# Window attention on one core: scores and transposes in smaller tiles of TensorE, a lag of three quarters, and two evacuations moved from VectorE to ScalarE

## The chip, the cores and the metric

The kernel runs on one core of a Trainium2 chip. The metric is the device time of one execution in microseconds (us). The kernel before takes 4781.35 us, the median of 3 runs (4780.85 to 4781.38).

## The reference

The input is 16 images of 56 x 56 places with 192 channels. Two residual layers follow one another, each on a group norm (32 groups) of its input. The first is a linear recurrence over 7 x 7 windows with a feed-forward of 768 channels; the change does not touch it. The second is shifted window attention, with 12 heads of 16 dimensions, 49 tokens to a window and 64 windows to an image:

```python
x = jnp.roll(x, (-s0, -s1), axis=(1, 2))
qkv = xw @ qkv_w.T + qkv_b
q, k, v = (qkv[0] * hd ** (-0.5), qkv[1], qkv[2])
attn = jnp.einsum('bhnd,bhmd->bhnm', q, k)
attn = attn + bias[None]          # relative position, then the shift mask
attn = jax.nn.softmax(attn, axis=-1)
out = jnp.einsum('bhnm,bhmd->bhnd', attn, v)
out = out @ proj_w.T + proj_b
```

## The kernel before

The attention works in units. A unit is a row of 8 windows of one image, so there are 128 units. A unit has four quarters p = 0 to 3, each of two windows w, laid in partitions 0 to 48 and 64 to 112 (SLOT = 64). Each engine runs the same order, written out by hand in its function `slot(i, c, r)`, joined by semaphores. The loop body holds two units (c = 0 and 1).

For a quarter, in words: **scores** (L1241) multiply queries `Q` by keys `Kp` into `ps_s`, for all heads of both windows. `Kp` is the keys spread out with zeros (block diagonal) by DMAs of SyncE (L840), so that one matmul serves several heads: four in the kernel before (HB = 4), whose 64 rows meet 4 x 49 = 196 columns. That makes 6 matmuls of a 64 x 64 tile of the array; the trace shows each fp32 matmul as two, so 12. VectorE scales them and adds the bias (L1097, into `L`), takes row maxima (L1101) and subtracts them for half the heads (L1111); GpSimd subtracts the other half (L888). ScalarE takes exponentials (L960, into `E`), VectorE the row sums and reciprocals (L1105, L1107), GpSimd multiplies (L882). Two quarters later (`lagged`) TensorE **transposes** the probabilities (L1249, 6 of 128 x 98 weights and 128 columns, both windows at once, into `ps_t`), ScalarE copies them out (L969, `PT`), TensorE multiplies them by the **values** (L1284, 98 x 32 tiles, 12 matmuls shown as 24, into `ps_v`) and ScalarE moves them out (L989, `oT`).

Between these TensorE has the work of the next unit v = u + 1 and of the last one u - 1: `turn` (L1180, transposes of the input, two halves h), `project` (L1192, queries and keys, steps 0, 1, 2 of 5 matmuls), `values` (L1204, two halves of 10) and `mix` (L1223, the output projection, two halves of 8). All share three PSUM banks `ps_w`, so each waits until its bank was read. The input parts `x_hi`, `x_lo` that `project` needs are made by ScalarE (`upper`, L930) and VectorE (`lower`, L1065). Step 0 of `project` yields keys and the last query channels; the latter are moved out by VectorE (`queries_b`, L1074), like half of the values (L1124).

TensorE's order in a unit is: p = 0: scores, transposes, mix 0, turn 0, values product, turn 1; p = 1: scores, transposes, project 0 and 1, values product; p = 2: scores, transposes, project 2, values 0, values product; p = 3: scores, transposes, values 1, values product, mix 1.

## Time and profile before

| | us |
|---|---|
| median of 3 runs | 4781.35 |
| the profiled execution | 4778.66 |
| its span, first to last instruction | 4776.7 |
| attention, first to last scores matmul | 2513 to 4759 |
| TensorE busy in the span | 4503.8 (94%) |
| VectorE busy | 3946.8 (83%) |
| ScalarE busy | 2366.2 (50%) |
| GpSimd busy | 2379.3 (50%) |

Starts in the timeline count from the first instruction. A matmul's duration runs from its start to its last result, so matmuls that follow each other overlap in the list: the pace of a group is read from starts, not from durations. Units are alike, so one unit of the steady stretch stands for all.

### The profile page before, as it was taken

Reading aid. Unit: us, or ns where it says so; the run is one execution under the profiler, and the core shown is the slowest. Engines: PE = TensorE matmul, PEld = TensorE weight load, DVE = VectorE, ACT = ScalarE, POOL = GpSimd, SP = SyncE. Lnnn points to the kernel's source line nnn. Section 1 sums busy time; section 2 is a strip of 40 time slices with the busy share of each in tenths; the row PEclk is TensorE's granted clock in tenths of the full one; section 3 lists DMA queues with packets and bytes.
Section 4 is the critical chain, followed back from the end, with each engine's and each line's share of the span. In section 5 each row is a group of like instructions: output and inputs, shape, how many; then the busy total and the mean of one; then the engine's idle time right before and its main releaser. Section 6 shows DMA issues by size and latency. Waiting matters only on the chain. (4 is left out here: it accounts for less than half of the span.)

```text
span 4776.7 us, 123308 instructions
## 1 busy us (share of the span) xinstructions
PE 4503.8 (94%) x42504; PEld 3833.8 (80%) x42504; DVE 3946.8 (83%) x7850; ACT 2366.2 (50%) x4594; POOL 2379.3 (50%) x2098
## 2 busy tenths in 40 slices
PE   0599999999999999999969999999999999999998
PEld 0488888888888888888857888888888888888887
DVE  6788888888888888888827888888888888888887
ACT  0244444444444444444415555555555656555565
POOL 1245554555555554555425555555555555555555
PEclk9999999999999999999969999999999999999999
DMA  8011111111111111111112222222222222222222
GB/s 341 21 38 39 39 41 38 38 39 39 41 37 39 39 41 37 39 40 41 34 40 67 69 68 69 69 67 71 67 70 69 68 68 69 70 68 70 67 70 59
DMA packets 397987, 285.95 MB, mean 60 GB/s; under 512 B 155355, under 2 KB 396235, under 8 KB 396747
## 3 DMA queue, kind: packets, MB, share of 16 engines
q1 hardware_dynamic: 395204, 283.19, 20.2%
q10 hardware_dynamic: 2736, 2.14, 0.1%
q8 instruction: 29, 0.48, 0.0%
q14 instruction: 18, 0.15, 0.0%
HBM read 120.34 MB, written 87.31 MB: 43 GB/s over the span
## 5 line engine op out<-in xcount | busy, mean ns | idle before, releaser
L882 POOL TENSOR_TENSOR E<-E,ri 128x588 f32<-128x588 f32 x512 | 646.3, 1262 | 1028.5 <-DVE ri L1107 1028.3
L602 PE MATMUL ps_o<-w,g_hi 128*128 128x384 f32 x2352 | 710.9, 365 | 5.9 <-DVE g_lo L542 4.1
L414 ACT ACTIVATE gF<-ps_g,b1f 128x512 f32<-128x512 f32 x588 | 404.7, 688 | 393.0 <-PE ps_g L633 390.7
L960 ACT ACTIVATE E<-L 128x588 f32<-128x588 f32 x512 | 356.1, 695 | 475.6 <-POOL L L888 242.5
L1097 DVE SCALAR_TENSOR_TENSOR L<-ps_s,bias 128x588 f32<-128x588 f32 x512 | 394.5, 770 | 178.0 <-PE ps_s L1241 161.9
L602 PE MATMUL ps_o<-w,g_lo 128*128 128x192 f32 x2352 | 534.8, 254 | 0.0
L1249 PE MATMUL ps_t<-ident,E 128*98 128x128 f32 x3072 | 441.3, 280 | 41.1 <-POOL E L882 41.1
L441 POOL TENSOR_TENSOR res<-xt,b2b 128x768 f32<-128x768 f32 x98 | 181.5, 1852 | 591.1 <-DVE x L490 591.1
L400 ACT ACTIVATE h_hi<-ps_h,hbias 128x512 fp32r<-128x512 f32 x196 | 123.1, 679 | 703.7 <-PE ps_h L617 703.7
L1249 PEld LDWEIGHTS ps_t<-ident,E 128*98 128x98 f32 x3072 | 313.4, 127 | 195.4 <-POOL E L882 108.3
L1241 PE MATMUL ps_s<-Kp,Q 64*64 64x196 f32 x6144 | 455.4, 342 | 2.7 <-DMA Kp<-K 2.7
L602 PEld LDWEIGHTS ps_o<-w,g_hi 128*128 128x128 f32 x2352 | 429.7, 189 | 26.6 <-issue 24.7
L602 PEld LDWEIGHTS ps_o<-w,g_lo 128*128 128x128 f32 x2352 | 444.0, 191 | 0.0
L1101 DVE TENSOR_REDUCE mx<-L 128x12 f32<-128x588 f32 x512 | 392.2, 766 | 17.5
L989 ACT ACTIVATE oT<-ps_v,vb 128x98 f32<-128x98 f32 (+1 forms) x1024 | 289.1, 334 | 234.6 <-PE ps_v L1284 228.7
L1105 DVE TENSOR_REDUCE sm<-E 128x12 f32<-128x588 f32 x512 | 387.8, 757 | 12.6 <-ACT E L960 1.4
L1223 PE MATMUL ps_w<-wp,oT 128*98 128x192 f32 x2048 | 385.4, 331 | 1.1 <-ACT oT L989 0.7
L1284 PEld LDWEIGHTS ps_v<-PT,Vx 98*32 98x32 f32 x12288 | 291.2, 150 | 92.9 <-issue 63.9
L1284 PE MATMUL ps_v<-PT,Vx 98*32 98x49 f32 x12288 | 351.4, 232 | 12.7 <-issue 3.9
L419 ACT ACTIVATE g_hi<-gF 128x512 fp32r<-128x512 f32 x588 | 355.4, 621 | 0.0
L451 POOL TENSOR_TENSOR g_lo<-gF,g_hi 128x512 fp32r<-128x512 f32 x196 | 250.5, 1299 | 197.3 <-ACT g_hi L419 197.3
L888 POOL TENSOR_TENSOR L<-L,mx 128x294 f32<-128x294 f32 x512 | 345.2, 674 | 6.1 <-DVE mx L1101 6.1
(211 smaller groups left out, 12090.5 us busy)
## 6 DMA issues: line engine op xcount, KB each, us to landing
xs<-in_x SPq DMA_DIRECT2D x8, 4704.0 KB, 22.0
xt<-in_x SPq DMA_DIRECT2D x98, 384.0 KB, 3.4
x_cells<-x SPq DMA_DIRECT2D x784, 48.0 KB
xb<-x_cells SPq DMA_DIRECT2D x128, 294.0 KB
Vx<-V SPq DMA_DIRECT2D x512, 73.5 KB
out<-yo SPq DMA_DIRECT2D x128, 294.0 KB
Kp<-K SPq DMA_DIRECT2D x512, 49.0 KB, 1.9
Kp<-K SPq DMA_DIRECT2D x512, 24.5 KB, 1.8
```

What stands on the lines that cost most here:

```text
L414: act.activation(gF[f % 4][:, :], ps_g[:, f % 2, :], ACT.Gelu, bias=b1f[:, f:f + 1]).then_inc(s_gelu, 1)
L419: act.activation(g_hi[:, g, :], gF[g % 4][:, :], ACT.Copy).then_inc(s_gh, 1)
L602: last = pe.matmul(dst, g[:, f, P * k:P * (k + 1)], w, start=(f == 0 and i == 0), stop=(f == FT - 1 and i == 1))
L882: pool.tensor_tensor(e, e, ri[p][:, :].unsqueeze(2).to_broadcast([P, HEADS, T]), ALU.mult)\
L960: act.activation(E[pp][:, :, :], L[pp][:, :, :], ACT.Exp).then_inc(s_ex, 1)
L1097: dve.scalar_tensor_tensor(out=L[p][:, :, :].rearrange("p (a h) m -> p a (h m)", a=3), in0=s_block(slice(0, 3)), scalar=HD ** -0.5, in1=ta ...
L1101: dve.tensor_reduce(mx[p][:, :], L[p][:, :, :], AX.X, ALU.max).then_inc(s_mx, 1)
L1105: dve.tensor_reduce(sm[pp][:, :], E[pp][:, :, :], AX.X, ALU.add).then_inc(s_sm, 1)
L1223: last = pe.matmul(ps_w(OUT1 if half else OUT0)[0:T2, C * a:C * (a + 1)], oT[d][p][:, k, :], wp[:, k, :], start=(k == 0), stop=(k == 1))
L1241: last = pe.matmul(s_block(b)[SLOT * w:SLOT * (w + 1)], Q[c][rows, chunk, 2 * p + w, :], Kp[c][rows, chunk, :, 2 * p + w, :], start=True, ...
L1249: last = pe.transpose(ps_t[0:T2, j // JB, P * (j % JB):P * (j % JB + 1)], E[lp][:, 2 * j:2 * j + 2, :].rearrange("p h m -> p (h m)"), iden ...
L1284: last = pe.matmul(ps_v[row:row + 2 * HD, col:col + T], Vx[lc][0:T2, 2 * lp + w, j:2 * HD * JP:JP], PT[lp % 2][0:T2, j, T * w:T * (w + 1)] ...
```

## The change

The head pairs become the unit of the scores: HB = 2, so a scores matmul has 32 rows of weights and 98 columns, and there are 12 for a quarter (24 in the trace) in tiles of 32 x 64. They come in two parts: pairs at places 0, 3, 1, 4 ahead of the transposes, and those at 2, 5 after them, behind a wait for the first part (`s_scx`). The transposes are split by window: 12 with 64 rows, 98 weight columns and 64 columns each. The heads lie in the order PAIR_AT in the logits and in the values product, whose loop now takes pairs 0, 4, 2, 1, 5, 3 and with them the column groups 0, 0, 2, 1, 1, 3 of the array, where it took 0, 1, 2, 3, 0, 1. The lag from scores to transposes is three quarters. `queries_b` and the copy of values half 0 go from VectorE to ScalarE. ScalarE copies `PT` ahead of the exponentials, VectorE subtracts maxima ahead of the row sums, GpSimd does `less_max` ahead of `norm`. `turn` 0 and 1 stand together in p = 0, `mix` 0 moves to p = 2, `project` 1 behind the values product of p = 1, `project` 2 and `values` 0 behind that of p = 2. The bank numbers of `ps_w` and the waits on them follow.

```diff
+PAIR_AT = (0, 4, 2, 1, 5, 3)
-HB = HEADS // 3
-QB = 256
+HB = 2
+SB = HEADS // 2 * T
-OUT0, TURN, QK, VAL, OUT1 = 0, 1, 3, 6, 8
+LAG = 3
+TURN, KEYS, OUT0, QRY, VAL, OUT1 = 0, 2, 4, 5, 6, 8
+def ps_qk(step):
+    return ps_w(QRY if step == 2 else KEYS + step)
-    return ps_s[:, :, :].rearrange("p a (b n) -> p (a b) n", n=QB)[:, b, 0:HB * T]
+def s_pair(j):
+    return ps_s[:, 2 * j // JP, T2 * (j % (JP // 2)):T2 * (j % (JP // 2) + 1)]
-    return (u, c, p - 2) if p >= 2 else (u - 1, 1 - c, p + 2)
-    return (64 * (b // 2), b % 2)
+    return (u, c, p - LAG) if p >= LAG else (u - 1, 1 - c, p + UP - LAG)
+    return slice(2 * HD * (g % PA), 2 * HD * (g % PA + 1)), g // PA
...
+            if is_unit(u):
+                less_max(u, p)
             if is_unit(pu):
                 norm(pu, pp)
-            if is_unit(u):
-                less_max(u, p)
...
+    def queries_b(i, c):
+        v = 2 * i + c + 1
+        full = ps_qk(0)[:, 0:UW].rearrange("p (w t) -> p w t", t=T)
+        upto(act, s_sc, UP * (v - 1))
+        act.activation(Q[1 - c][0:CB, 1, :, 0:T], full[CB:P], ACT.Identity,
+                       bias=par[1 - c][CB:P, 3:4]).then_inc(s_qb, 1)
...
-            if is_unit(pu):
-                k = UP * u + p - 1
-                act.wait_ge(s_sub, k + 1)
-                act.wait_ge(s_sbp, k + 1)
-                upto(act, s_pt, k - 3)
-                act.activation(E[pp][:, :, :], L[pp][:, :, :], ACT.Exp).then_inc(s_ex, 1)
+            lu, lc, lp = lagged(u, c, p)
+            k = UP * u + p - LAG
             if nxt and p == 2:
                 evacuated(i, c, 1)
-            lu, lc, lp = lagged(u, c, p)
-            k = UP * u + p - 2
             if is_unit(lu):
                 act.wait_ge(s_pt, k + 1)
                 upto(act, s_pv, k - 1)
-                act.activation(PT[lp % 2][0:T2, :, :].rearrange("p (a b) (w t) -> p a (b w) t", a=2, w=2),
-                               ps_t[0:T2, :, 0:JB * P].rearrange("p a (n t) -> p a n t", t=SLOT)[:, :, :, 0:T],
+                act.activation(PT[lp % 2][0:T2, :, :].rearrange("p j (w t) -> p w j t", w=2),
+                               ps_t[0:T2, :, 0:JP * SLOT].rearrange("p w (j t) -> p w j t", t=SLOT)[:, :, :, 0:T],
                                ACT.Copy).then_inc(s_ptc, 1)
-            if nxt and p == 1:
-                evacuated(i, c, 0)
-            if nxt and p == 2:
-                evacuated(i, c, 2)
-            if nxt and p == 3:
-                act.wait_ge(s_v, 2 * (u + 1) + 2)
-                copied(act, i, c)
-                act.activation(V[0:T2, 2:4, :], v_sum(1), ACT.Copy).then_inc(s_vc[1], 1)
-            if nxt and p == 0:
-                upper(i, c, 0)
+            if is_unit(pu):
+                act.wait_ge(s_sub, UP * u + p)
+                act.wait_ge(s_sbp, UP * u + p)
+                upto(act, s_pt, UP * u + p - 4)
+                act.activation(E[pp][:, :, :], L[pp][:, :, :], ACT.Exp).then_inc(s_ex, 1)
+            if nxt:
+                if p == 0:
+                    upper(i, c, 0)
+                    upper(i, c, 1)
+                if p == 1:
+                    evacuated(i, c, 0)
+                    queries_b(i, c)
+                if p == 3:
+                    act.wait_ge(s_v, 2 * (u + 1) + 2)
+                    copied(act, i, c)
+                    act.activation(V[0:T2, 0:2, :], v_sum(0), ACT.Copy).then_inc(s_vc[0], 1)
+                    act.activation(V[0:T2, 2:4, :], v_sum(1), ACT.Copy).then_inc(s_vc[1], 1)
             if is_unit(lu):
...
-            if nxt and p == 0:
-                upper(i, c, 1)
+            if nxt and p == 2:
+                evacuated(i, c, 2)
...
-        dve.tensor_scalar(Q[1 - c][0:CB, 1, :, 0:T], full[CB:P], par[1 - c][CB:P, 3:4], None,
...
-            if is_unit(pu):
-                dve.wait_ge(s_ex, k)
-                dve.tensor_reduce(sm[pp][:, :], E[pp][:, :, :], AX.X, ALU.add).then_inc(s_sm, 1)
-                dve.wait_ge(s_sm, k)
-                dve.reciprocal(ri[pp][:, :], sm[pp][:, :]).then_inc(s_ri, 1)
             if is_unit(u):
                 dve.wait_ge(s_mx, k + 1)
                 l = L[p][:, 0:HS, :]
                 dve.tensor_tensor(l, l, mx[p][:, 0:HS].unsqueeze(2).to_broadcast([P, HS, T]),
                                   ALU.subtract).then_inc(s_sub, 1)
-            if is_unit(u - 1) and p == 0:
-                finish(i, c, 0)
             if nxt and p == 0:
                 lower(i, c, 0)
                 lower(i, c, 1)
-            if nxt and p == 1:
-                queries_b(i, c)
-            if nxt and p == 2:
-                dve.wait_ge(s_v, 2 * (u + 1) + 1)
-                copied(dve, i, c)
-                dve.tensor_copy(V[0:T2, 0:2, :], v_sum(0)).then_inc(s_vc[0], 1)
+            if is_unit(pu):
...
+            if is_unit(u - 1) and p == 2:
+                finish(i, c, 0)
...
+    def scores(c, p, places):
+        for j in places:
+            rows, chunk = pair_rows(PAIR_AT[j])
+            for w in range(2):
+                last = pe.matmul(s_pair(j)[SLOT * w:SLOT * (w + 1)], Q[c][rows, chunk, 2 * p + w, :],
+                                 Kp[c][rows, chunk, :, 2 * p + w, :], start=True, stop=True)
+        return last
...
-        if h == 0:
-            pe.wait_ge(s_xb[d], 16 * LOADS * (i + c + 1))
-            upto(pe, s_vc[1], v)
-        else:
-            if isinstance(v, int):
-                upto(pe, s_yo, 2 * (v - 2))
...
             pe.wait_ge(s_xl, 2 * v + 2)
-            upto(pe, s_yo, 2 * (v - 2) + 1)
+            upto(pe, s_yo, 2 * (v - 2))
+        if step == 2:
+            pe.wait_ge(s_qkm, 3 * v + 1)
+            pe.wait_ge(s_qb, v + 1)
...
-        pe.wait_ge(s_qkm, 3 * v + half + 1)
         if half == 0:
-            pe.wait_ge(s_qb, v + 1)
+            pe.wait_ge(s_qkm, 3 * v + 2)
+        else:
+            upto(pe, s_yo, 2 * (v - 2) + 1)
...
+        if is_unit(v + 2):
+            if half == 0:
+                pe.wait_ge(s_xl, 2 * (v + 2) + 2)
+            else:
+                pe.wait_ge(s_qkm, 3 * (v + 2) + 3)
+        else:
+            pe.wait_ge(s_vc[1], UNITS)
+            pe.wait_ge(s_qkm, 3 * UNITS)
             pe.wait_ge(s_yo, 2 * v)
-        elif half == 0:
-            pe.wait_ge(s_vc[0], v + 2)
-        else:
-            pe.wait_ge(s_qkm, 3 * (v + 2) + 3)
...
-            if is_unit(u):
-                k = UP * u + p
-                if isinstance(u, int):
-                    upto(pe, s_lg, k)
-                for w, b in ((0, 0), (0, 2), (1, 0), (1, 2), (0, 1), (1, 1)):
-                    row, chunk = key_block(b)
-                    rows = slice(row, row + HB * HD)
-                    last = pe.matmul(s_block(b)[SLOT * w:SLOT * (w + 1)], Q[c][rows, chunk, 2 * p + w, :],
-                                     Kp[c][rows, chunk, :, 2 * p + w, :], start=True, stop=True)
-                last.then_inc(s_sc, 1)
+            k = UP * u + p - LAG
             if is_unit(lu):
-                k = UP * u + p - 2
                 pe.wait_ge(s_nm, k + 1)
                 upto(pe, s_ptc, k)
+            if is_unit(u):
+                if p == 0:
+                    pe.wait_ge(s_qkm, 3 * u + 3)
+                    pe.wait_ge(s_qb, u + 1)
+                    pe.wait_ge(s_kp[c], 16 * K_SPREADS * (i + 1))
+                upto(pe, s_lg, UP * u + p)
+                scores(c, p, (0, 3, 1, 4)).then_inc(s_scx, 1)
+            if is_unit(lu):
                 for j in range(JP):
-                    last = pe.transpose(ps_t[0:T2, j // JB, P * (j % JB):P * (j % JB + 1)],
-                                        E[lp][:, 2 * j:2 * j + 2, :].rearrange("p h m -> p (h m)"),
-                                        ident[:, :])
+                    for w in range(2):
+                        rows = slice(SLOT * w, SLOT * (w + 1))
+                        last = pe.transpose(ps_t[0:T2, w, SLOT * j:SLOT * (j + 1)],
+                                            E[lp][rows, 2 * j:2 * j + 2, :].rearrange("p h m -> p (h m)"),
+                                            ident[rows, rows])
                 last.then_inc(s_pt, 1)
-            if is_unit(u - 1) and p == 0:
+            if nxt and p == 0:
+                pe.wait_ge(s_xb[1 - c], 16 * LOADS * (i + c + 1))
+                for h in range(2):
+                    upto(pe, s_vc[h], v)
+            if is_unit(u):
+                pe.wait_ge(s_scx, UP * u + p + 1)
+                scores(c, p, (2, 5)).then_inc(s_sc, 1)
+            if is_unit(u - 1) and p == 2:
                 mix(i, c, 0)
             if nxt:
+                if p == 0:
+                    turn(i, c, 0)
+                    turn(i, c, 1)
                 if p == 1:
...
-                if p == 2:
-                    project(i, c, 2)
                 if p == 3:
                     values(i, c, 1)
-            if nxt and p == 0:
-                turn(i, c, 0)
-            if nxt and p == 1:
-                project(i, c, 1)
-            if nxt and p == 2:
-                values(i, c, 0)
             if is_unit(lu):
-                k = UP * u + p - 2
-                if is_unit(u):
-                    pe.wait_ge(s_lg, UP * u + p + 1)
-                if p == 0 and nxt:
-                    upto(pe, s_yo, 2 * (u - 1))
...
-                        row, col = 2 * HD * (j % PA), T2 * (j // PA) + T * w
+                        g = PAIR_AT[j]
+                        row, col = 2 * HD * (g % PA), T2 * (g // PA) + T * w
                         last = pe.matmul(ps_v[row:row + 2 * HD, col:col + T],
-                                         Vx[lc][0:T2, 2 * lp + w, j:2 * HD * JP:JP],
+                                         Vx[lc][0:T2, 2 * lp + w, g:2 * HD * JP:JP],
...
-            if nxt and p == 0:
-                turn(i, c, 1)
-            if nxt and p == 3:
-                pe.wait_ge(s_qkm, 3 * (u + 1) + 3)
-                pe.wait_ge(s_qb, u + 2)
-                pe.wait_ge(s_kp[1 - c], 16 * K_SPREADS * (i + c + 1))
+            if nxt:
+                if p == 1:
+                    project(i, c, 1)
+                if p == 2:
+                    project(i, c, 2)
+                    values(i, c, 0)
...
-    def by_dimension(block):
-        return CB * block + np.array([HD * e + d for d in range(HD) for e in range(CB // HD)])
-    first, second = np.r_[by_dimension(0), by_dimension(2)], by_dimension(1)
+    by_dimension = np.array([2 * HD * g + HD * e + d for g in range(JP) for d in range(HD) for e in range(2)])
+    first, second = by_dimension[0:P], by_dimension[P:C]
```

## Rows read from the trace of the kernel before

**Rows 1.** The page: span, and busy time of each engine.

```profile
span 4776.7 us, 123308 instructions
...
PE 4503.8 (94%) x42504; PEld 3833.8 (80%) x42504; DVE 3946.8 (83%) x7850; ACT 2366.2 (50%) x4594; POOL 2379.3 (50%) x2098
```

**Rows 2.** Windows view: busy time of each engine, granted clock, DMA share, GB/s.

```profile
3000.00:3400.00 400.00, 391.72 (x5154) 329.28 (x5158) 327.74 (x590) 238.37 (x500) 217.11 (x228) 1.00 0.24 68
```

**Rows 3.** Timeline of TensorE: start, us from first start to last end, operation, count.

```profile
3003.15 1.54 PE L1223 MATMUL ps_w<-wp,oT 128*98 128x192 f32 x8
3004.62 0.89 PE L1241 MATMUL ps_s<-Kp,Q 64*64 64x196 f32 x12
3005.44 0.86 PE L1249 MATMUL ps_t<-ident,E 128*98 128x128 f32 x6
3006.14 1.46 PE L1223 MATMUL ps_w<-wp,oT 128*98 128x192 f32 x8
3007.44 0.50 PE L1180 MATMUL ps_w<-ident,xb 98*128 98x98 f32 x4
3007.87 0.68 PE L1284 MATMUL ps_v<-PT,Vx 98*32 98x49 f32 x24
3008.48 0.53 PE L1180 MATMUL ps_w<-ident,xb 98*64 98x98 f32 x4
3008.94 0.89 PE L1241 MATMUL ps_s<-Kp,Q 64*64 64x196 f32 x12
3009.76 0.86 PE L1249 MATMUL ps_t<-ident,E 128*98 128x128 f32 x6
3010.56 0.44 PE L1192 MATMUL ps_w<-x_hi,wqkv_a_hi 128*128 128x392 f32 x1
...
3012.54 0.69 PE L1284 MATMUL ps_v<-PT,Vx 98*32 98x49 f32 x24
3013.16 0.89 PE L1241 MATMUL ps_s<-Kp,Q 64*64 64x196 f32 x12
3014.36 0.86 PE L1249 MATMUL ps_t<-ident,E 128*98 128x128 f32 x6 [0.31 <-POOL E L882]
```

**Rows 4.** The same timeline: first scores of the next two units.

```profile
3022.29 0.89 PE L1241 MATMUL ps_s<-Kp,Q 64*64 64x196 f32 x12
...
3039.81 0.89 PE L1241 MATMUL ps_s<-Kp,Q 64*64 64x196 f32 x12
```

**Rows 5.** Lines in 3000:3173, durations in ns: minimum/median/maximum.

```profile
L1249 PE MATMUL ps_t<-ident,E x237: 272/273/318, 3000.7 to 3173.0; 128*98 128x128 f32 x119
...
L1284 PE MATMUL ps_v<-PT,Vx x936: 220/224/264, 3002.5 to 3171.3; 98*32 98x49 f32 x188
...
L1223 PE MATMUL ps_w<-wp,oT x160: 326/326/406, 3003.2 to 3165.7; 128*98 128x192 f32 x160
```

**Rows 6.** Waits in 3000:3173 (ten units): us in total, times, longest.

```profile
PE ps_t L1249 <- POOL E L882: 3.1, 10, 0.3
```

**Rows 7.** Timeline of VectorE in the first quarter of the unit.

```profile
3005.55 0.77 DVE L1097 SCALAR_TENSOR_TENSOR L<-ps_s,bias 128x588 f32<-128x588 f32 x1 [0.27 <-PE ps_s L1241]
3006.36 0.77 DVE L1101 TENSOR_REDUCE mx<-L 128x12 f32<-128x588 f32 x1
...
3007.97 0.40 DVE L1111 TENSOR_TENSOR L<-L,mx 128x294 f32<-128x294 f32 x1
3008.29 0.55 DVE L1086 TENSOR_TENSOR yo<-ps_w,rs 98x384 f32<-98x384 f32 x1
...
3009.81 0.62 DVE L1065 SCALAR_TENSOR_TENSOR x_hi<-ps_w,par,x_hi 64x392 fp32r<-64x392 f32 x1 [0.44 <-ACT x_hi L930]
```

**Rows 8.** Timeline of ScalarE and GpSimd there.

```profile
3005.49 0.70 ACT L960 ACTIVATE E<-L 128x588 f32<-128x588 f32 x1 [1.67 <-POOL L L888]
3006.42 0.66 ACT L969 ACTIVATE PT<-ps_t 98x588 f32<-98x588 f32 x1 [0.23 <-PE ps_t L1249]
...
3010.00 1.84 POOL L903 TENSOR_TENSOR rs<-xb,pbb 98x768 f32<-98x768 f32 x1
```

More of the change, by code:

```diff
@@ L760, in build @@
             s_vx = [sem(f"v_spread{b}") for b in range(2)]
-            s_sc, s_lg, s_mx = sem("scores_summed"), sem("logits"), sem("row_maxima")
+            s_scx, s_sc, s_lg, s_mx = sem("scores_first_rows_summed"), sem("scores_summed"), sem("logits"), sem("row_maxima")
             s_sub, s_sbp = sem("maxima_off_first_heads"), sem("maxima_off_last_heads")
@@ L1188, in project @@
                         pe.wait_ge(s_xl, 2 * v + 2)
-                        upto(pe, s_yo, 2 * (v - 2) + 1)
+                        upto(pe, s_yo, 2 * (v - 2))
+                    if step == 2:
+                        pe.wait_ge(s_qkm, 3 * v + 1)
+                        pe.wait_ge(s_qb, v + 1)
                     terms = W_QKV.terms(x_hi, x_lo, slice(P * m, P * (m + 1)))
                     for k, (w, x) in enumerate(terms):
-                        last = pe.matmul(ps_w(QK + step)[:, 0:UW], w, x, start=(k == 0), stop=(k == len(terms) - 1))
+                        last = pe.matmul(ps_qk(step)[:, 0:UW], w, x, start=(k == 0), stop=(k == len(terms) - 1))
                     last.then_inc(s_qk, 1)
@@ L1379 @@
     arrays["proj_b"] = plain("L1_conv_proj_b")
-    arrays["rpb"] = plain("L1_conv_rpb_table")
+    arrays["rpb"] = np.ascontiguousarray(plain("L1_conv_rpb_table")[:, [2 * g + e for g in PAIR_AT for e in range(2)]])
     arrays.update(shape_constants())
```

38 lines of the change are left out of this document (14 added, 24 removed).

## The prediction

> **What bounds the kernel now.** I read the page first: TensorE is busy for 94% of the span, VectorE for 83%, ScalarE and GpSimd for 50% [rows 1]. The page is an average over two layers, so next comes the windows view of the attention alone: in 400 us TensorE is busy for 391.7, VectorE for 327.7, ScalarE for 238.4, GpSimd for 217.1, at a granted clock of 1.00, which is the 2.4 GHz level [rows 2]. So TensorE sets the pace, but busy time can hide empty places in the array. For that I read TensorE's timeline over a unit, by starts. Two units take 35.19 us (3004.62 to 3039.81), 17.67 and 17.52, mean 17.59 [rows 3, 4]; there are 128.
>
> Three things are to be seen in it. First, the pace of a group. Transposes: (0.86 - 0.32)/5 = 0.109 us for 128 columns; input transposes: (0.50 - 0.25)/3 = 0.083 for 98 columns. So a column of a fp32 pass costs 0.85 ns. The 12 scores matmuls of 196 columns run four at a time, in four waves: 0.82 us from their start to the next start [rows 3]. Second, the seams. After the same work, mix with its neighbours in the same tile shape takes 1.30 us (3006.14 to 3007.44), and 1.47 with another shape on either side (3003.15 to 3004.62) [rows 3]. The first mix matmul after a seam lasts 406 ns where its median is 326 [rows 5]: 0.08 is the first weight load, which no matmul covers, and the remaining 0.09 is the array running empty. I take 0.094 for that empty stretch at each change of shape, and for the first load 0.053 (scores; 0.82 - 4 x 0.166 - 0.094 gives 0.05 to 0.06), 0.045 (transposes, 318 - 273), 0.04 (values product, 264 - 224), 0.08 (mix) [rows 5] and, for the 128 columns of project, 0.11, an estimate from mix by columns. Third, the waits. In the third quarter scores to transposes takes 1.20 us instead of 0.82, for GpSimd's normalised probabilities, once a unit [rows 3, 6]. In the second quarter transposes to project takes 0.80 (3009.76 to 3010.56), some 0.18 over what its six matmuls take, for VectorE's `lower`, whose last ends at 3010.43 [rows 3, 7]. With smaller ones I count 0.64 of waits, and 16.95 of TensorE's own work, in a unit.
>
> **The change, part by part.** All counts are for a unit.
>
> *Scores.* 98 columns cost 0.083 a wave. The first part has 16 matmuls in four tiles, four waves; the second 8, two waves: 6 x 0.083 = 0.50 against 4 x 0.166 = 0.66. Four times -0.166: -0.66. Tiles in two row halves and two column halves already run together (the scores), so I expect it of 32-row tiles as well.
>
> *Transposes.* Twelve, two at a time if the row halves run together, so six waves. What a wave of 64 columns costs, no row shows. Streaming gives 64 x 0.85 = 0.055 as the lower end. The values product streams only 49 columns (0.042), but its busiest column group starts 8 matmuls in 0.68 - 0.22 = 0.46 us, the first load of 0.04 among it: 0.060 each [rows 3, 5]; that is the nearest row. The upper end with pairs running together is 0.083, the pace at which the input transposes pass. I take 0.060: 6 x 0.060 = 0.36 against 6 x 0.109 = 0.654, four times -0.294: -1.18.
>
> *Seams.* Before there were 14 changes of shape: 4, 3, 3 and 4 in the quarters, since transposes, project, values and mix share one shape. Now transposes have a shape of their own, the second scores follow them, and the values product has project, values or mix behind it in three quarters: 5 + 6 + 6 + 6 = 23. Nine more: +0.85. First loads: before 4 x 0.053 + 4 x 0.045 + 4 x 0.04 + 0.03 (turn 1) + 0.08 (mix 1) = 0.66; after 8 x 0.053 + 4 x 0.045 + 4 x 0.04 + 0.053 (turn) + 3 x 0.11 (project) + 3 x 0.08 (values 1, mix 0 and 1) = 1.39. +0.72.
>
> *Values product.* Same 24 matmuls, but the column groups now come as 0, 0, 2, 1, 1, 3. Before, 24 matmuls of 0.22 started within 0.46 us [rows 3, 5], so four groups do overlap in that order; for the new one there is no row. If the order mattered not at all the cost is 0; if a group's four had to start before the next group gets its turn, about 0.12. I take 0.05, near the trace's good overlap, four times: +0.20.
>
> TensorE's own work: -0.66 - 1.18 + 0.85 + 0.72 + 0.20 = -0.07, so 16.88. The smaller tiles gain little: the seams take back what streaming gives.
>
> *Waits that go.* With a lag of three the transposes take probabilities that GpSimd finished a step earlier; 0.38 goes. What is late next on that path: the last quarter's normalisation. It ends 2.4 after `lower` does (row sums and reciprocal about 1, GpSimd's multiply 1.26 and hand-overs), and is wanted by the scores of the third quarter 2.9 after it (project, values product, project again), so it holds by 0.5. The reading of logits is also relaxed: before, the values product waited for it, now only the next scores do, more than 1 us later. The values product of p = 0 wants `PT`: 0.12 + 0.66 + 0.12 after the transposes' last result [rows 3, 8], some 1.06 from their last column; TensorE has 1.2 of scores, seams and turns before it. Covered, narrowly.
>
> *The wait that stays.* Project 0 needs `lower` 1. Now both turns stand behind the second scores, and on VectorE `lower` stands behind logits, maxima and subtraction. From the scores' last result: 0.04 + 0.77 + 0.04 + 0.77 + 0.04 + 0.40 - 0.08 + 0.62 - 0.08 + 0.62 + 0.12 = 3.26 [rows 3, 7]; a result comes 0.16 after the last column, so 3.42 from there. ScalarE is not later: `PT` 0.66, exponentials 0.70 and two `upper` of 0.59 end before VectorE wants them. TensorE meanwhile has 0.094 of seam, turns 0.81, values product 0.66, scores 0.49, transposes 0.50, scores 0.32: 2.87. It waits 0.55, where all waits together were 0.64. While it waits, the rest of the project chain is queued behind it, and nothing else can run.
>
> *Moved work.* ScalarE gains two operations of some 0.5 to 0.6 and goes from 60% to about 66% of the stretch [rows 2]; VectorE loses as much. Neither bounds. `queries_b` on ScalarE stands between exponentials and `oT` of p = 1, which the values product of p = 2 wants 3 us later. The key spreads move the same bytes in half the DMAs, and their readers are 9 us away. The addition for the residual (1.84 on GpSimd [rows 8]) now stands behind a later `norm` and delays `less_max` of p = 1; the exponentials of p = 2 meet it with about no slack, and their readers have 1 us. The wait `s_scx` is covered by the transposes (0.5 against the 0.16 that a result takes); only the first three quarters of all lack that cover, below 1 us. The end of the kernel stays bound by the last normalisation.
>
> **The sum.** 16.88 + 0.55 = 17.43, and the first quarter's transposes, which are ahead of the chain that TensorE waits for, are in both; a unit goes from 17.59 to 17.42, -0.17, times 128 = -22 us. The profiled execution took 4778.7 (4776.7 of span and 2.0 around it), so 4757 on its terms; the median of the runs is 2.7 higher. I give **4758**.
>
> What a unit is worth: one ns in the pace of the transposes costs 6 x 3 = 18 ns (the second quarter's are hidden by the wait), so at 0.055 it is 4747, at 0.060 it is 4758, at 0.070 there is nothing left, and at 0.083 it is 4811.
>
> **The rivals.**
>
> *Weight loads bound the transposes (slower).* Twelve loads of 98 weight columns take the place of six, each under 64 columns instead of 128. If a load takes the 0.08 that mix shows for 98 columns [rows 5], pairs pass every 0.083: +0.023 x 18 = +0.41, net +0.24 a unit, +31: **4811**. It decides from 0.070. For it: the load is now longer than the streaming that has to cover it. Against: the first transposes last only 0.045 longer than the rest, with the same 98 columns. The Trainium skill, "TensorE: Matmul & The Clock Gate", section "LDWEIGHTS (loading the stationary operand)", says that a load's time is its columns divided by 1.2 GHz, whatever the rows. For 98 columns that is an estimate of 82 ns, and by it this rival would be the forecast. Mix agrees with it (80 ns), the fp32 transposes do not (45 ns). Chance 0.20.
>
> *The row halves do not run together (slower).* Twelve single passes of 0.060 in place of six: +0.36 in three quarters, +1.08, less the gain 0.17: +0.9 a unit, **4897**. No row shows 64 x 128 tiles; scores show that two row halves do. It would also hold if a small tile did nothing it says. Chance 0.05.
>
> *The seams are smaller or VectorE's chain shorter (faster).* If TensorE did not wait for `lower`, 17.42 - 0.55 = 16.87: -92, **4689**. The order in VectorE's program and its durations speak against it. Half of it, 4735, is possible. Chance 0.12.
>
> *The gain goes elsewhere (no change).* Another wait takes 0.1 to 0.2: the values product at 0.12 rather than 0.05 (+0.21 in three quarters), or the exponentials behind GpSimd's residual addition. **4781**. Chance 0.18.
>
> **How the numbers follow.** Forecast 0.45 (its own range 4740 to 4770), the rivals as above. The range runs from 4710 to 4825; outside are the separate row halves and a wait that vanishes whole. A measurement tells about 0.2%, 9.6 us, from no change. Faster by more than that: 0.55; within: 0.16; slower: 0.29.
>
> **What would show it.** In the timeline of after: transposes x12 from first to last start within 0.35 us (if 0.45 or more, the load rival; 0.65, the halves); seams of 0.25 us between last start and next start on both sides of them; values product 0.66 to the next start; project 0 starting 0.12 behind `lower`, with an idle of about 0.5; no wait on GpSimd by transposes or scores; a unit of 17.4. It is wrong if TensorE waits elsewhere, or if a unit without waits is not near 16.9.

## The result and the profile after

The kernel after takes **4773.0 us** (median; 4769.1 to 4775.4) beside 4781.5 for the one before (4780.0 to 4782.7): a ratio of 0.9981 with an interval of 0.9975 to 0.9988. That is 8.4 us less, just within the 0.2% that the prediction called no change; it had 23 us less. The profiled execution took 4771.5, its span is 7.0 us shorter than before.

The page and the windows view answer to [rows 1] and [rows 2]:

```profile
span 4769.7 us, 140614 instructions
...
PE 4464.8 (94%) x51720; PEld 3768.6 (79%) x51720; DVE 4038.5 (85%) x7594; ACT 2472.6 (52%) x4850; POOL 2481.5 (52%) x2098
```

```profile
3000.00:3400.00 400.00, 384.47 (x6797) 317.42 (x6797) 345.08 (x548) 257.39 (x548) 236.65 (x229) 1.00 0.25 69
```

VectorE lost two operations, yet it is busy for 17 us more in 400 (experiment six tells why). TensorE's timeline, of the first and second quarter of a unit and then of the next unit's first, shows what became of its work, and it answers to [rows 3]:

```profile
3004.06 0.57 PE L1170 MATMUL ps_s<-Kp,Q 32*64 32x98 f32 x16
3004.56 0.54 PE L1253 MATMUL ps_t<-ident,E 64*98 64x64 f32 x12
3005.03 0.40 PE L1170 MATMUL ps_s<-Kp,Q 32*64 32x98 f32 x8
3006.11 0.44 PE L1194 MATMUL ps_w<-x_hi,wqkv_a_hi 128*128 128x392 f32 x1 [0.68 <-DVE x_hi L1078]
...
3007.19 0.73 PE L1284 MATMUL ps_v<-PT,Vx 98*32 98x49 f32 x24
3007.85 0.45 PE L1194 MATMUL ps_w<-x_hi,wqkv_a_hi 128*128 128x392 f32 x1
...
3018.85 0.57 PE L1170 MATMUL ps_s<-Kp,Q 32*64 32x98 f32 x16
3019.35 0.54 PE L1253 MATMUL ps_t<-ident,E 64*98 64x64 f32 x12
3019.82 0.40 PE L1170 MATMUL ps_s<-Kp,Q 32*64 32x98 f32 x8
3020.15 0.89 PE L1179 MATMUL ps_w<-ident,xb 98*128 98x98 f32 x8
3020.97 0.73 PE L1284 MATMUL ps_v<-PT,Vx 98*32 98x49 f32 x24
3021.63 0.57 PE L1170 MATMUL ps_s<-Kp,Q 32*64 32x98 f32 x16
```

By starts: the first part of the scores takes 0.50, the transposes 0.47, the second part 0.33 (3019.82 to 3020.15), the turns 0.82, the values product 0.66. From the second part to project 0 it is 1.08 (3005.03 to 3006.11): 0.33 of work and 0.75 of waiting. Over 80 steady units a unit takes 17.578, where before it took 17.603 by the same count. So TensorE's own work is 17.58 - 0.75 = 16.83 (forecast 16.88) and the wait is 0.75 (forecast 0.55). The work is as foreseen, the wait is not. The twelve transposes start within 0.32 (0.54 less the 0.22 that the last one lasts), as the prediction's sign had it. From the last of these starts to the scores it is 0.15 (3019.67 to 3019.82): a pace of 0.056 and an empty stretch of 0.09. The 0.25 that the prediction named for this place does not follow from its own terms. VectorE's timeline shows the chain that ends the wait, and answers to [rows 7]:

```profile
3002.72 0.77 DVE L1101 SCALAR_TENSOR_TENSOR L<-ps_s,bias 128x588 f32<-128x588 f32 x1 [0.77 <-PE ps_s L1170]
3003.52 0.77 DVE L1105 TENSOR_REDUCE mx<-L 128x12 f32<-128x588 f32 x1
3004.32 0.47 DVE L1109 TENSOR_TENSOR L<-L,mx 128x294 f32<-128x294 f32 x1
3004.70 0.62 DVE L1078 SCALAR_TENSOR_TENSOR x_lo<-ps_w,par,x_hi 128x392 fp32r<-128x392 f32 x1
3005.36 0.62 DVE L1078 SCALAR_TENSOR_TENSOR x_hi<-ps_w,par,x_hi 64x392 fp32r<-64x392 f32 x1
...
3008.52 1.88 DVE L1109 TENSOR_TENSOR L<-L,mx 128x294 f32<-128x294 f32 x1
```

From the start of logits to the end of the second `lower` it takes 3.26; the prediction's terms give 3.10 for that. The subtraction is 0.47, not 0.40, and its successor starts 0.38 behind it instead of 0.32; the second `lower` starts 0.66 behind the first, not 0.54: no overlap there. The trace of before had a row for that. The `lower` that starts at 3009.81 and lasts 0.62 [rows 7] is followed 0.65 later, without overlap, by:

```profile
3010.46 0.77 DVE L1097 SCALAR_TENSOR_TENSOR L<-ps_s,bias 128x588 f32<-128x588 f32 x1
```

**Where the 7.0 us of span come from.** About half is the steady units' 0.025 each. The rest lies at the two ends, as the logits of the first quarter show. In VectorE's timeline of before, then of after, those of units 0 and 2 are:

```profile
2514.11 0.77 DVE L1097 SCALAR_TENSOR_TENSOR L<-ps_s,bias 128x588 f32<-128x588 f32 x1 [3.92 <-PE ps_s L1241]
...
2547.66 0.77 DVE L1097 SCALAR_TENSOR_TENSOR L<-ps_s,bias 128x588 f32<-128x588 f32 x1 [0.26 <-PE ps_s L1241]
```

```profile
2514.34 0.77 DVE L1101 SCALAR_TENSOR_TENSOR L<-ps_s,bias 128x588 f32<-128x588 f32 x1 [8.38 <-PE ps_s L1170]
...
2545.85 0.77 DVE L1101 SCALAR_TENSOR_TENSOR L<-ps_s,bias 128x588 f32<-128x588 f32 x1 [0.77 <-PE ps_s L1170]
```

After is 0.2 late in unit 0, 1.8 early in unit 2, 5.5 early in the last unit (4748.35 and 4742.84) and 7.0 at the end. So 2.0 are gained once in the first two units and 1.5 once behind the last unit's start. The prediction had neither. In the first two units the granted clock is not at its 2.4 GHz level all the time: over 2515 to 2520 its mean is 0.50 before and 0.71 after. How much of the 2.0 is the clock was not separated.

### The profile page after: what moved, and what is told of

It reads as the page before. It is cut to its first block and busy times, and to the rows that moved or that the text cites. A ratio compares the mean times of both kernels' runs of the same rounds, so it can differ in the third digit from the quotient of the medians.

```text
span 4769.7 us, 140614 instructions
## 1 busy us (share of the span) xinstructions
PE 4464.8 (94%) x51720; PEld 3768.6 (79%) x51720; DVE 4038.5 (85%) x7594; ACT 2472.6 (52%) x4850; POOL 2481.5 (52%) x2098
## 5 line engine op out<-in xcount | busy, mean ns | idle before, releaser
L887 POOL TENSOR_TENSOR E<-E,ri 128x588 f32<-128x588 f32 x512 | 601.5, 1175 | 410.4 <-DVE ri L1119 410.4
L893 POOL TENSOR_TENSOR L<-L,mx 128x294 f32<-128x294 f32 x512 | 483.4, 944 | 511.7 <-DVE mx L1105 511.7
L976 ACT ACTIVATE PT<-ps_t 98x588 f32<-98x588 f32 x512 | 342.7, 669 | 461.4 <-PE ps_t L1253 451.3
L1101 DVE SCALAR_TENSOR_TENSOR L<-ps_s,bias 128x588 f32<-128x588 f32 x512 | 384.1, 750 | 230.8 <-PE ps_s L1170 230.8
L1170 PE MATMUL ps_s<-Kp,Q 32*64 32x98 f32 x12288 | 494.0, 259 | 1.5 <-POOL E L887 0.6
L1109 DVE TENSOR_TENSOR L<-L,mx 128x294 f32<-128x294 f32 x512 | 417.2, 815 | 17.4
L1227 PE MATMUL ps_w<-wp,oT 128*98 128x192 f32 x2048 | 396.3, 337 | 0.7 <-ACT oT L1002 0.7
L1170 PEld LDWEIGHTS ps_s<-Kp,Q 32*64 32x64 f32 x12288 | 297.5, 130 | 125.4 <-issue 65.2
L1284 PEld LDWEIGHTS ps_v<-PT,Vx 98*32 98x32 f32 x12288 | 310.6, 151 | 99.8 <-issue 64.0
L1284 PE MATMUL ps_v<-PT,Vx 98*32 98x49 f32 x12288 | 374.7, 235 | 2.8 <-ACT PT L976 2.8
```

The lines of the kernel that those rows point to most:

```text
L887: pool.tensor_tensor(e, e, ri[p][:, :].unsqueeze(2).to_broadcast([P, HEADS, T]), ALU.mult)\
L893: pool.tensor_tensor(l, l, mx[p][:, HS:HEADS].unsqueeze(2).to_broadcast([P, HEADS - HS, T]), ALU.subtract).then_inc(s_sbp, 1)
L1101: dve.scalar_tensor_tensor(out=L[p][:, :, :].rearrange("p (a h) m -> p a (h m)", a=2), in0=ps_s[:, :, 0:SB], scalar=HD ** -0.5, in1=tab, o ...
L1109: dve.tensor_tensor(l, l, mx[p][:, 0:HS].unsqueeze(2).to_broadcast([P, HS, T]), ALU.subtract).then_inc(s_sub, 1)
L1170: last = pe.matmul(s_pair(j)[SLOT * w:SLOT * (w + 1)], Q[c][rows, chunk, 2 * p + w, :], Kp[c][rows, chunk, :, 2 * p + w, :], start=True, s ...
L1227: last = pe.matmul(ps_w(OUT1 if half else OUT0)[0:T2, C * a:C * (a + 1)], oT[d][p][:, k, :], wp[:, k, :], start=(k == 0), stop=(k == 1))
```

## The experiments

The kernel before took 4781.4, 4781.9 and 4777.7 beside the three groups of runs (one to four; five to eight; nine and ten). No edit changes what is computed.

**One: the input parts ahead of the subtraction.** If the wait before project 0 is VectorE's chain, taking the subtraction out of it must give its 0.4 to 0.5.

```diff
+            if nxt and p == 0:
+                lower(i, c, 0)
+                lower(i, c, 1)
             if is_unit(u):
                 dve.wait_ge(s_mx, k + 1)
...
-            if nxt and p == 0:
-                lower(i, c, 0)
-                lower(i, c, 1)
```

> The changed kernel with one thing moved: on VectorE both lower parts of the next unit's input stand ahead of the subtraction of the maxima in the first quarter. Theory (the 0.75 us that TensorE idles before project 0, once a unit, is VectorE's chain logits, maxima, subtraction, lower 0, lower 1): the subtraction's 0.47 leaves the chain, the idle falls from 0.75 to about 0.27, a unit from 17.58 to 17.10, the time by 61 us to about 4712. Rival (the idle only covers something else that is late, such as the exponentials or the normalised probabilities): a new wait takes its place, less than 10 us gained.

Measured: **4712.5** (4707.3 to 4713.9), 0.9857 [0.9842, 0.9872]; a unit of 17.083. TensorE's timeline, the second scores and project 0:

```profile
3005.19 0.40 PE L1170 MATMUL ps_s<-Kp,Q 32*64 32x98 f32 x8
3005.77 0.44 PE L1194 MATMUL ps_w<-x_hi,wqkv_a_hi 128*128 128x392 f32 x1 [0.18 <-DVE x_hi L1078]
```

0.58 in place of 1.08, with the same TensorE program: the wait is that chain. Moving three lines is worth 60 us, seven times the whole change. The 0.25 of wait that is left ends with the same chain.

**Two: values product by column groups.** The prediction guessed 0.05 for the order 0, 0, 2, 1, 1, 3. Here it is 0, 1, 2, 3, 0, 1 again, over the same data.

```diff
-                for j in range(JP):
-                    g = PAIR_AT[j]
+                for g in range(JP):
+                    j = PAIR_AT.index(g)
```

> The changed kernel with the values product taken again in the order of column groups 0, 1, 2, 3, 0, 1. Theory (the new order costs 0.05 us each time, because matmuls of one column group stand behind each other at the head of TensorE's queue): from its start to the next start 0.61 instead of 0.66, in three quarters of a unit (in the first the wait before project 0 takes it up), -0.15 a unit, -19 us, about 4754. Rival (the order is free, and the 0.66 has another cause such as the place of its operands): 0.66 stays, no change.

Measured: **4758.3** (4755.8 to 4758.8), 0.995 [0.9937, 0.9964]. TensorE's timeline in the second quarter:

```profile
3004.04 0.69 PE L1284 MATMUL ps_v<-PT,Vx 98*32 98x49 f32 x24
3004.66 0.45 PE L1194 MATMUL ps_w<-x_hi,wqkv_a_hi 128*128 128x392 f32 x1
```

0.61 to the next start where after has 0.66: 0.047 for 24 matmuls. Three of four such gains count (the one of the first quarter is eaten by the wait): 3 x 0.047 x 128 = 18; measured 15. The steady units do give it: 17.434 for 17.578, 0.144 less. But three units of the profiled execution take 18.77, and in each of them TensorE's granted clock leaves its 2.4 GHz level in project 0, straight behind the wait. For one of them the windows view (PE, PEld, DVE, ACT, POOL, then the clock) and TensorE's timeline:

```profile
3574.00:3583.00 9.00, 8.27 (x142) 6.54 (x144) 8.00 (x12) 6.12 (x13) 5.52 (x6) 0.81 0.24 66
```

```profile
3578.26 0.57 PE L1194 MATMUL ps_w<-x_hi,wqkv_a_hi 128*128 128x392 f32 x1 [0.73 <-DVE x_hi L1078]
```

Project 0 takes 1.81 there instead of 1.09, and 1.34 are lost in all before the clock is back; three times that is 4 us.

**Three: both.**

> Both of the above in one kernel. Theory: TensorE's own work 0.20 less, and project 0 starts 0.48 earlier behind the scores of the first quarter: -0.63 a unit, -80 us, about 4693. Rival (TensorE is then held by GpSimd's normalised probabilities or by the copy PT): less than the two apart together, 4715 or more.

Measured: **4688.2** (4687.1 to 4690.7), 0.9807 [0.9794, 0.982]; a unit of 16.937, of which 0.29 are still the wait before project 0. One and two give 60 and 15, together they give 85: behind one the reordering is worth 0.146 a unit, three times 0.047 and the same as alone. No unit of three has a lowered clock.

**Four: both evacuations on VectorE again.** Evacuations are the moves out of PSUM, here `queries_b` and half of the values. The prediction costed their move to ScalarE at nothing. On VectorE they stand behind the row sums, and leave ScalarE's program.

```diff
+            if nxt and p == 1:
+                queries_b(i, c)
+            if nxt and p == 3:
+                dve.wait_ge(s_v, 2 * (u + 1) + 1)
+                copied(dve, i, c)
+                dve.tensor_copy(V[0:T2, 0:2, :], v_sum(0)).then_inc(s_vc[0], 1)
```

> The changed kernel with the last query channels (second quarter) and half of the values (fourth quarter) moved out by VectorE again, behind its row sums. Theory (neither engine bounds; what counts is only the chain in the first quarter, which has neither): within 6 us of the changed kernel, 4767 to 4779. Rival (VectorE, busy 86% of the stretch, is what gives the pace, and the relief of 1.2 us a unit pays): 17.58 rises by 0.3 or more, 4810 or more.

Measured: **4783.7** (4777.1 to 4787.3), 1.0002 [0.9993, 1.0011]; 10.7 above after, 5 more than the theory allowed. A unit is 0.036 longer, 4.6 us, nearly all of it a wait of TensorE's `values` 1 for VectorE's `yo`. The rest is not in the steady units. The profiled execution, the slowest of eleven, is 6.6 behind after at unit 2 already, 11.2 in the last unit and 15.8 at the end. At both ends its granted clock is lower: 0.50 over 2535 to 2540 where after has 1.00, and 0.50 over 4760 to 4770 where after has 0.99. Whether the edit brings that about, or these executions had it by chance, no run shows. So the move to ScalarE is worth 4.6 us in waits and 10.7 by the medians.

**Five: whole transposes in the new places.** This gives the price of a small transpose by itself.

```diff
-                    for w in range(2):
-                        rows = slice(SLOT * w, SLOT * (w + 1))
-                        last = pe.transpose(ps_t[0:T2, w, SLOT * j:SLOT * (j + 1)],
-                                            E[lp][rows, 2 * j:2 * j + 2, :].rearrange("p h m -> p (h m)"),
-                                            ident[rows, rows])
+                    last = pe.transpose(ps_t[0:T2, j // JB, P * (j % JB):P * (j % JB + 1)],
+                                        E[lp][:, 2 * j:2 * j + 2, :].rearrange("p h m -> p (h m)"),
+                                        ident[:, :])
```

> The changed kernel with the transposes whole again: 6 of 128 rows and 128 columns a quarter in place of 12 of 64 rows and 64 columns, in the same place between the two parts of the scores. Theory (each quarter's split transposes save 6 x 0.109 - 12 x 0.028 = 0.32 us of TensorE; in the second quarter the wait before project 0 hides it): from their start to the next start 0.79 instead of 0.47, a unit from 17.58 to 18.54, +123 us, about 4896. Rival (the gain of the split is given back by the extra changes of shape, which whole transposes between two scores have as well, so it is not seen): less than +60.

Measured: **4893.6** (4892.2 to 4895.2), 1.0235 [1.0219, 1.025]. TensorE's timeline, and the durations of the small transposes in after (minimum/median/maximum in ns):

```profile
3005.32 0.86 PE L1251 MATMUL ps_t<-ident,E 128*98 128x128 f32 x6
3006.11 0.40 PE L1170 MATMUL ps_s<-Kp,Q 32*64 32x98 f32 x8
```

```profile
L1253 PE MATMUL ps_t<-ident,E x468: 216/216/262, 3001.8 to 3168.0; 64*98 64x64 f32 x156
```

0.79 against 0.47. Three times 0.32 is 0.96, and the unit is 0.95 longer; the fourth shortens the wait before project 0 to 0.43. Twelve small ones start in pairs every (0.54 - 0.262)/5 = 0.056: neither the load rival (0.083) nor the one of separate halves (twice 0.060) holds. The Trainium skill, "TensorE: Matmul & The Clock Gate", section "LDWEIGHTS (loading the stationary operand)", gives a load its columns divided by 1.2 GHz, by its figures an estimate of 82 ns for 98. Mix agrees [rows 5]; these transposes do not, at 56 ns a pair.

**Six: GpSimd apart from VectorE.** In after, the subtraction of the second quarter lasts 1.88 (above, 3008.52) where it lasts 0.47 elsewhere. Does that cost anything? `less_max` waits for the subtraction, and the residual addition goes ahead of `norm` in the second quarter.

```diff
+                pool.wait_ge(s_sub, UP * u + p + 1)
...
-            if is_unit(pu):
-                norm(pu, pp)
-            if is_unit(u) and p == 0:
+            if is_unit(u) and p == 1:
...
+            if is_unit(pu):
+                norm(pu, pp)
```

> The changed kernel with GpSimd kept off VectorE's subtraction: its own subtraction waits for VectorE's, and the residual addition comes behind it in the second quarter instead of the first. Theory (the two engines exclude each other while both read two tensors of SBUF, which stretches VectorE's subtraction from 0.47 to 1.88 in the second quarter and GpSimd's from 0.68 to 0.95, but none of that is on the path to project 0): the operations go back to 0.47 and 0.68, and the time stays within 6 us of 4773. Rival (this stretching holds the pace): 15 us or more faster.

Measured: **4774.3** (4770.4 to 4775.5), 0.9984 [0.9975, 0.9993]. GpSimd's and VectorE's timelines:

```profile
3011.18 1.17 POOL L887 TENSOR_TENSOR E<-E,ri 128x588 f32<-128x588 f32 x1
3012.82 0.68 POOL L894 TENSOR_TENSOR L<-L,mx 128x294 f32<-128x294 f32 x1 [0.47 <-DVE L L1110]
```

```profile
3011.62 1.05 DVE L1110 TENSOR_TENSOR L<-L,mx 128x294 f32<-128x294 f32 x1
3017.03 0.47 DVE L1110 TENSOR_TENSOR L<-L,mx 128x294 f32<-128x294 f32 x1
```

`less_max` is back from 0.96 to 0.68, and the subtraction is 0.47 except where it still meets `norm`. The time is the same: the meeting is real and lies off the path. In after the subtractions are busy for 75.2 us of 400, before for 36.1, more than the 26 us of the two operations that left. The 0.47 within the chain is not from such a meeting, for it is 0.47 with GpSimd idle too (here at 3017.03, where GpSimd does nothing until 3017.64). It goes by what stands ahead on VectorE, as seven shows.

**Seven: the whole input chain first** (on top of three), to see what is late next. ScalarE does `upper` ahead of the exponentials; VectorE goes from logits straight to `lower`, then maxima, sums and subtraction.

```diff
+            if nxt and p == 0:
+                upper(i, c, 0)
+                upper(i, c, 1)
...
-                dve.tensor_reduce(mx[p][:, :], L[p][:, :, :], AX.X, ALU.max).then_inc(s_mx, 1)
             if nxt and p == 0:
                 lower(i, c, 0)
                 lower(i, c, 1)
+            if is_unit(u):
+                dve.tensor_reduce(mx[p][:, :], L[p][:, :, :], AX.X, ALU.max).then_inc(s_mx, 1)
```

> The kernel with both edits (lower parts first, values product by column group) carried further: in the first quarter ScalarE makes the upper parts ahead of the exponentials, and VectorE does logits, lower 0, lower 1, maxima, row sums, reciprocals, subtraction. Theory (the last 0.29 us before project 0 is the same chain, which now ends before TensorE is ready; the normalised probabilities then arrive just in time for the third quarter): 16.94 to 16.64 a unit, -38 us, about 4650. Rival (GpSimd's normalisation of the last quarter takes the place of the wait): 4675 or more, with an idle of TensorE before the scores of the third quarter.

Measured: **4664.5** (4663.1 to 4665.4), 0.9754 [0.9741, 0.9767], between its theory and its rival. The wait before project 0 is gone, and a unit is 16.739: 16.64 of work and 0.10 of a new wait, of the third quarter's scores for GpSimd's `norm`, which the later exponentials have moved (from project 1 to these scores it is 1.19 where it was 1.09). The waits view has it for the weight loads, which wait longer than the matmuls behind them, over ten units (total, times, longest):

```profile
PEld ps_s L1177 <- POOL E L887: 3.9, 11, 0.4
```

VectorE's timeline has the subtraction in both lengths, behind the maxima and behind a reciprocal:

```profile
3010.03 0.47 DVE L1119 TENSOR_TENSOR L<-L,mx 128x294 f32<-128x294 f32 x1
...
3016.75 0.23 DVE L1115 RECIPROCAL ri<-sm 128x12 f32<-128x12 f32 x1
3016.89 0.40 DVE L1119 TENSOR_TENSOR L<-L,mx 128x294 f32<-128x294 f32 x1
```

The one at 3010.03 stands straight behind the maxima. The one at 3016.89 stands behind a reciprocal, as in before, and its successor starts 0.32 later. In after the subtraction stands straight behind the maxima. So the order that the change chose made it 0.07 longer.

**Eight: a lag of two** with all else as in after (`LAG = 2`).

> The changed kernel with a lag of two quarters, all else as it is. Theory (in the new order scores wait for the probabilities of the quarter that is transposed next, and with two quarters these are finished only after the scores could start: by the trace of the changed kernel 3.7 us late in the third quarter, 1.2 in the fourth): 3.7 to 6 us more a unit, 5250 to 5550. Rival (a lag of two suffices, and the third quarter of lag buys only the 0.38 us that the kernel before waited): 4830 or less.

Measured: **5820** (5806 to 5831), 1.2161 [1.2143, 1.218], far above both expectations. The theory (scores stand behind a wait for `norm`) is right in kind. The long waits stand before the scores of the first quarter (1.46) and of the second (3.37), not where the theory put them. TensorE's timeline, and the windows view:

```profile
3016.87 0.57 PE L1170 MATMUL ps_s<-Kp,Q 32*64 32x98 f32 x16 [1.46 <-POOL E L887]
...
3023.92 0.93 PE L1170 MATMUL ps_s<-Kp,Q 32*64 32x98 f32 x16 [3.37 <-POOL E L887]
```

```profile
3000.00:3400.00 400.00, 309.74 (x4692) 250.77 (x4688) 219.52 (x377) 178.17 (x378) 162.77 (x157) 0.83 0.17 47
...
3016.80:3018.10 1.30, 1.23 (x36) 1.01 (x36) 0.00 (x0) 0.07 (x1) 0.00 (x0) 1.00 0.41 103
3018.10:3019.60 1.50, 1.50 (x16) 1.21 (x8) 1.26 (x2) 1.50 (x3) 0.00 (x0) 0.52 0.61 163
```

The same 16 matmuls take 0.57 and 0.93. The granted clock is at its 2.4 GHz level up to 3018.10, 1.2 us after the wait of 1.46 has ended, and then falls while TensorE is busy; it is 0.50 all through the wait of 3.37. Over 400 us its mean is 0.83, where after has 1.00. The waits view counts 37.4 us of waiting for `norm` in 173, which is 5.5 in a unit of 25.66. A unit is 8.1 longer than in after. Waiting has grown by 4.8 of these, inside the 3.7 to 6 expected; the other 3.3 is by this count an estimate of what the clock costs. What the run shows is that this order of work needs the lag of three.

**Nine: values product last in every quarter** (on top of seven), behind the lines below instead of ahead of them. With project, values or mix ahead of it, three changes of shape and their first loads should go, and its values have more time.

```diff
+            if nxt:
+                if p == 1:
+                    project(i, c, 1)
+                if p == 2:
+                    project(i, c, 2)
+                    values(i, c, 0)
+            if is_unit(u - 1) and p == 3:
+                mix(i, c, 1)
```

> The kernel of the input-first run, with the values product as the last thing TensorE does in every quarter, so that project 1, project 2 with values 0, and mix 1 join the full-shape work ahead of it. Theory (each change of shape costs 0.094 us of empty array and the next group's first load): three changes and three first loads of 0.08 to 0.11 fewer, -0.58 a unit of TensorE's own work; 0.2 of it is spent waiting for GpSimd's normalised probabilities before the scores of the third quarter, which now come earlier: -0.38, 16.74 to 16.36, about 4616. Rival (the shape changes cost nothing that matters, the time follows VectorE and ScalarE): within 10 us of 4664.

Measured: **4653.7** (4651.2 to 4654.1), 0.9738 [0.9725, 0.9751]: the fastest kernel here, 2.6% below the one before beside it. Of the expected 48 it gave 11. TensorE's own work did fall, from 16.64 to 16.08 a unit. That is 0.56 for an expected 0.58, and the test of the prices of a seam and of a first load. But the waits rose from 0.10 to 0.58:

```profile
3007.84 0.57 PE L1177 MATMUL ps_s<-Kp,Q 32*64 32x98 f32 x16 [0.39 <-issue]
...
3014.76 0.57 PE L1177 MATMUL ps_s<-Kp,Q 32*64 32x98 f32 x16 [0.23 <-POOL E L887]
...
3024.29 0.57 PE L1177 MATMUL ps_s<-Kp,Q 32*64 32x98 f32 x16
```

Three waits make them up. The one for `norm` before the third quarter's scores (3014.76) is 0.28 by starts, about what was expected. One of 0.07 stands before `values` 1, for VectorE's `yo`. And 0.22 stands before the first quarter's scores, in every second unit only: 0.39 at 3007.84, nothing at 3024.29. These last two are the 37 us that are missing. Units take some 16.45 and 16.86 by turns. The loop body holds two units, and the trace has the loop's branch on TensorE's sequencer (L788) at 3006.9, just ahead of the longer wait. In after, `mix` 1 stands there, 1.47 us of queued work; here it is the values product, 0.61. That the branch is what the scores wait for fits these places, but no run moves it.

So from here half of the waiting is the softmax chain through VectorE, ScalarE and GpSimd, and over a third stands at the turn of the loop.

**Ten: row sums and `norm` first** (on top of nine), to shorten that chain in the first quarter: row sums and reciprocals ahead of the maxima on VectorE, `norm` ahead of `less_max` on GpSimd, the residual addition one quarter later. VectorE's part of the edit:

```diff
-            if is_unit(u):
-                dve.wait_ge(s_lg, k + 1)
-                dve.tensor_reduce(mx[p][:, :], L[p][:, :, :], AX.X, ALU.max).then_inc(s_mx, 1)
             if is_unit(pu) and p == 0:
...
+            if is_unit(u):
+                dve.wait_ge(s_lg, k + 1)
+                dve.tensor_reduce(mx[p][:, :], L[p][:, :, :], AX.X, ALU.max).then_inc(s_mx, 1)
```

> The same, with VectorE's row sums and reciprocals of the first quarter ahead of its maxima, GpSimd's normalisation ahead of its subtraction there, and its residual addition in the second quarter behind the normalisation. Theory (the wait before the scores of the third quarter is lower parts, maxima, row sums, reciprocals, normalisation, and loses the 0.7 of the maxima): no wait of TensorE is left, 16.06 to 16.15 a unit, 4578 to 4590. Rival (VectorE, with 14 to 15 us of work in a unit of 16, is now late somewhere else): 4605 or more, and the idle stands before scores or project of another quarter.

Measured: **4825.1** (4823.6 to 4827.4), 1.01 [1.0084, 1.0115]: 1% above the kernel before and 171 us above nine, as its rival had it. ScalarE's and GpSimd's timelines:

```profile
3021.99 0.69 ACT L988 ACTIVATE E<-L 128x588 f32<-128x588 f32 x1 [2.47 <-POOL L L893]
```

```profile
3019.88 1.17 POOL L887 TENSOR_TENSOR E<-E,ri 128x588 f32<-128x588 f32 x1 [4.21 <-DVE ri L1114]
3021.01 0.90 POOL L893 TENSOR_TENSOR L<-L,mx 128x294 f32<-128x294 f32 x1
```

GpSimd idles 4.21 for the reciprocals, and only then does `less_max`; the exponentials wait 2.47 for it, and the moves out of PSUM behind them on ScalarE are late. A unit is 17.90, and without its waits still 16.08, as expected. TensorE now waits in three other places, over ten units (total, times, longest):

```profile
PE ps_s L1179 <- DVE L L1103: 5.4, 10, 0.6
PE ps_w L1216 <- DVE yo L1092: 5.4, 10, 0.6
PE ps_s L1179 <- DMA Kp<-K: 4.6, 9, 0.6
```

The scores of the third quarter wait for VectorE's logits, `values` 1 for its `yo`, and the scores of the first quarter for the spread of the keys. The wait has changed its place, and grown.

## Why the prediction was off in size

*TensorE's own work, 16.88: right, 16.83 measured.* The pace of the transposes, taken at 0.060, is 0.056, and five confirms it: 4893.6 where 0.32 in three quarters gives 4896. The seams and first loads are tested by nine: three of each fewer, 0.56 for 0.58. The values product's order, a guess of 0.05, is 0.047 (two). The guess was lucky: the prediction had no row for it, between 0 and 0.12.

*Waits that go: right.* In the steady units no scores or transposes of after wait for GpSimd. The cover claimed for `PT`, for `s_scx` and for the last quarter's `norm` held.

*The wait that stays, 0.55: 0.75 measured.* This is the step that failed. Place, cause and what is queued behind it were right (one), but the chain on VectorE is 0.16 longer than its sum. 0.12 of that is an overlap of 0.08 between the two `lower`, where there is none (0.66 from start to start for 0.62 of length). It was read at another pair of operations, a subtraction and what follows it [rows 7]. The row of before for what follows a `lower` (0.65 for 0.62) was not used. 0.06 is the subtraction, taken at its length behind a reciprocal (0.40) for a place behind the maxima (0.47, seven). Two hand-overs within the chain give 0.02 back. The remaining 0.04 are at the chain's two ends, as far as the hundredths allow: project 0 starts 0.13 behind the end of `lower` (3005.98 to 3006.11) for 0.12, and logits start some 0.22 behind the last column of the scores for 0.20. TensorE's cover of 2.87 was right.

*The sum.* A unit lost 0.025, where the forecast had it lose 0.17 (17.578 for 17.42; before is 17.603 for 17.59). The difference is some 19 us. The two ends gave 3.8 of span that the sum did not have: 4758 + 19 - 4 = 4773. That this comes out to the microsecond is luck: 4781.35 less the forecast's own 21.8 is 4759.6, not 4758, and the medians differ by 1.3 more than the profiled executions. In the faster rival, half of the wait gone would be 4723; 4735 is half of its gain over before.

*Moved work, costed at nothing: wrong by 5 to 10 us* (four), and hidden in the result by the larger miss. The residual addition behind `norm` cost nothing: moved off VectorE's subtraction (six), the time is the same, though in after it stretches operations.

*Rivals.* The load rival and the separate halves are out (five). "The gain goes elsewhere" came nearest in time, but not by what it named: neither the values product nor the exponentials took it. The faster rival, no wait for `lower`, was not what happened, yet its price was about right: with the wait gone and the values product reordered (seven) a unit's work is 16.64, against 16.83 - 4 x 0.047 = 16.64.

## What to carry to other kernels

When a change saves on the bounding engine and lengthens what it waits for, the result is a small difference of large terms: here, in the prediction's terms, -1.84 of streaming, +1.57 of seams and loads and +0.20 of order, and +0.11 of waiting as measured (0.75 for its 0.64). Then the longest chain on the other engine deserves the same care as the engine itself, pair by pair, with an overlap granted only where a row shows that pair. A length or an overlap is that of an operation in its place: it can change with what stands ahead. And look in that chain for work that the waiting engine does not need: three lines moved gave seven times what the retiling did. After two such moves other waits came up, one of them at the turn of the loop, where the reordering had left little queued work.

## What the runs showed of the hardware

Two operations of VectorE and GpSimd that both read two tensors from SBUF exclude each other: the subtraction that started at 3008.52 ended at 3010.40, 0.33 after GpSimd's residual addition, which ran from 3008.25 to 3010.07:

```profile
3008.25 1.82 POOL L908 TENSOR_TENSOR rs<-xb,pbb 98x768 f32<-98x768 f32 x1
3010.04 0.90 POOL L893 TENSOR_TENSOR L<-L,mx 128x294 f32<-128x294 f32 x1
```

The Trainium skill, "SBUF — State Buffer", section "SBUF: two separate sides", says that the pair of ports they share is a lock for a whole instruction; the trace agrees, and six shows both at their own length once apart (0.47 and 0.68).

The order of column groups costs time even where all four are used: 24 matmuls in 0.61 as 0, 1, 2, 3, 0, 1 and in 0.66 as 0, 0, 2, 1, 1, 3 (two). And 64-row tiles run in pairs at 0.056 a pair, with 98 columns of weights each (five).

An operation on VectorE has one length or another by what stands ahead of it: the same subtraction takes 0.40 behind a reciprocal and 0.47 behind the maxima (seven), and a `lower` is followed without overlap (0.66 and 0.65 for 0.62).

The granted clock can fall while TensorE is busy, some time after it idled: in two in project 0 behind an idle of 0.72 or 0.73, in three units of 128, and in eight 1.2 us after one of 1.46. After idles 0.68 in the same place once a unit, and its clock stays at 1.00 over the steady 400 us.
